# A latent attention's layer norm moved into the next stage's projection block, with contexts through a ring of three buffers

## The reference

```python
def _layernorm(x): (x - mean) * rsqrt(var + 1e-5)                     # no affine part

# fourth stage
x = _layernorm(x + latent_attention(x))

# fifth stage, its projections
q     = rms_norm(linear(x, q_w, q_b), norm_q_w)                       # x: 800 rows of 512
k     = rms_norm(linear(ctx_txt, k_w, k_b), norm_k_w)                 # context rows 257 to 360 of 8 batches
k_img = rms_norm(linear(ctx_img, k_img_w, k_img_b), norm_k_img_w)     # context rows 0 to 256
# then attention(q, k_img, v_img) + attention(q, k, v)

# sixth stage's weights, in bf16
scale = clip(mean(|w_g|), 1e-8)             # over 64 weights
q3    = clip(round(w_g / scale), -1, 1)
w     = w + (q3 * scale - w)                # both roundings to bf16 are kept
```

## Time and profile before

| | |
|---|---|
| median of 3 runs | 2397.46 us (2393.82 to 2399.54) |
| the profiled execution's own time | 2400.9 us |
| its span | 2399.2 us, 36927 instructions |
| TensorE matmul busy | 2210.1 us (92%) |
| VectorE, ScalarE, GpSimd busy | 1451.4, 1179.4, 471.3 us |

### The profile page before, as it was taken

How to read it: one execution, slowest core, us unless ns; L and a number is a source line. 1 busy time by engine, 2 the same in 40 slices (tenths; PEclk the granted TensorE clock), 3 DMA queues, 4 the chain that set the end, 5 groups by cost and what they waited for, 6 DMA issues and landing times. The chain is left out here.

```text
span 2399.2 us, 36927 instructions
## 1 busy us (share of the span) xinstructions
PE 2210.1 (92%) x13440; PEld 1735.9 (72%) x13440; DVE 1451.4 (60%) x3971; ACT 1179.4 (49%) x3034; POOL 471.3 (20%) x386
## 2 busy tenths in 40 slices
PE   7998899999998999899987988999996797998998
PEld 4643788888887888788876965665664594665987
DVE  2275677777776777677767535455553356883434
ACT  1052667576765676566752324452352244772222
POOL 0220122222221212122211002223232000221433
PEclk9999999999999999999998999999997998998999
DMA  6001211111101111111003023213220700002300
GB/s 230 1 34 66 76 36 36 36 37 36 37 35 37 36 37 34 38 36 36 10 5 141 1 73 119 96 72 115 102 75 27 250 1 19 2 2 87 125 1 28
DMA packets 46316, 135.58 MB, mean 57 GB/s; under 512 B 5527, under 2 KB 23959, under 8 KB 41143
## 3 DMA queue, kind: packets, MB, share of 16 engines
q1 hardware_dynamic: 34328, 112.00, 12.8%
q0 software_dynamic: 2304, 12.58, 1.3%
q10 hardware_dynamic: 9504, 8.65, 1.2%
HBM read 113.07 MB, written 20.15 MB: 56 GB/s over the span
## 5 line engine op out<-in xcount | busy, mean ns | idle before, releaser
L775 PE MATMUL psum<-qa_kv_raw,context 128*128 128x256 f32 (+1 forms) x1536 | 343.6, 380 | 0.0
L775 PEld LDWEIGHTS psum<-qa_kv_raw,context 128*128 128x128 f32 (+1 forms) x1536 | 277.2, 184 | 44.9
L761 PE MATMUL psum<-qa_w,qa_xq 128*100 128x256 bf16 (+1 forms) x3072 | 271.6, 249 | 19.1 <-issue 16.0
L761 PEld LDWEIGHTS psum<-qa_w,qa_xq 128*100 128x100 bf16 x3072 | 259.9, 128 | 21.0 <-issue 20.7
L877 ACT ACTIVATE qa_prob<-psum,qa_nm 100x361 f32<-100x361 f32 x128 | 71.8, 561 | 173.4 <-DVE qa_nm L1011 173.4
L1103 POOL TENSOR_TENSOR qa_w<-qa_w_raw,qa_w 128x768 bf16<-128x768 f32 x32 | 52.6, 1643 | 447.4 <-DVE qa_w L953 447.4
L973 DVE BATCH_NORM_STATS2 qa_st<-psum 100x6 f32<-100x128 f32 x320 | 69.6, 283 | 89.1 <-PE psum L761 89.1
L2395 ACT ACTIVATE it_prob<-psum,it_nm 100x257 f32<-100x257 f32 (+1 forms) x256 | 101.7, 412 | 42.6 <-DVE it_nm L2419 42.6
L832 PE MATMUL psum<-qa_catq,qa_o 128*128 128x400 f32 x512 | 111.9, 361 | 9.9 <-DVE X L1050 6.0
L2082 POOL TENSOR_TENSOR la_gf_diff<-la_gf_what,la_gf_w 128x1536 bf16<-128x1536 bf16 x16 | 49.3, 3083 | 306.4 <-DVE la_gf_what L1991 266.0
L1002 DVE TENSOR_SCALAR qa_nrm_t<-psum,qa_mv,qa_sd 100x128 f32<-100x128 f32 x320 | 107.8, 403 | 2.4
(11 more groups left out here) (345 smaller groups left out, 5093.5 us busy)
## 6 DMA issues: line engine op xcount, KB each, us to landing
qa_w_raw<-in_qa_w SPq DMA_DIRECT2D x9, 1536.0 KB, 6.8
la_gf_raw<-in_gf_w SPq DMA_DIRECT2D x16, 768.0 KB, 4.3
gf_ternary<-gf_made POOLq DMA_DIRECT2D x16, 768.0 KB, 3.6
gf_w<-gf_ternary SPq DMA_DIRECT2D x4, 3072.0 KB, 24.4
qa_piece<-in_tf_pieces ACTq DMA_DIRECT2D x66, 128.0 KB, 2.1
qa_o_raw<-in_qa_o SPq DMA_DIRECT2D x8, 1024.0 KB, 5.0
context<-in_context SPq DMA_DIRECT2D x8, 722.0 KB, 12.4
it_context<-in_context SPq DMA_DIRECT2D x8, 722.0 KB, 11.3
```

The costliest lines, as they stand in the source:

```text
L761: mm = pe.matmul(psum[0:T, 2 + at // 512, at % 512:at % 512 + width], xq[:, kind, k, b * T:(b + 1) * T], w3[:, s, part, k, at:at + width], ...
L775: mm = pe.matmul(psum[0:rows, i // 2, (i % 2) * 256:(i % 2) * 256 + 256], ctxT[:, k, b * TC + t0:b * TC + t0 + rows], kv_raw[:, s, k, :], ...
```

## The change

The separate block `ln_la` is dropped. Its mean, centring, squares, variance, root, reciprocal and multiplication are written at the head of the image-text projections' block, over halves (products, root, reciprocal) and quarters (the rest), with the centring in place in Y and the squares in `qn`. The order of the groups becomes k0, k1, q of tokens 0 to 399, k2 to k7, q of tokens 400 to 599, q of tokens 600 to 799. The contexts go through three buffers; the load of context b waits until the products of context b - 3 are done. SyncE queues the image key weights, context 0, the text key weights, context 1, then the query weights. In the latent attention, set 2's three steps follow additions 0, 1 and 2, set 3's scales follow additions 2, 3 and 4 (with the magnitude products placed likewise), and set 3's steps follow additions 5, 6 and 7, in every quad. The last quad's GpSimd does three sets; the two passes and the store of the sixteenth set move into the projections' block, behind the clearing of a row of v. Buffers that outlive the latent attention are in `LastGated`. The rest of the diff's core:

```diff
-                    if i in (0, 1, 3):
-                        ternary(g, 2, steps=((0, 1, 3).index(i),))
-                    if i in (2, 4, 6):
-                        take_scale(g, 3, i // 2 - 1, 5)
-                ternary(g, 3)
+                    if i < 3:
+                        ternary(g, 2, steps=(i,))
+                    if i in (2, 3, 4):
+                        take_scale(g, 3, i - 2, 5)
+                    if i >= 5:
+                        ternary(g, 3, steps=(i - 5,))
...
-            quad(QUADS - 1)
+            quad(QUADS - 1, 3)
...
+    RING = 3
+    groups = [("k", 0, 0, TC), ("k", 1, 0, TC), ("q", 0, 0, HALF)] + [("k", b, 0, TC) for b in range(2, B)] + [
+        ("q", 1, 0, QUARTER), ("q", 1, QUARTER, HALF)]
...
+            def load_context(b):
+                if b >= RING:
+                    sp.wait_ge(S_["kq_mm"], (ordinal(b - RING) + 1) * C)
+                sp.dma_start(ctxT[:, b % RING, :, :], a["context"][b]).then_inc(c_in[b % RING], 16)
+
+            sp.dma_start(w[1][:, :, :], a["it_ki"]).then_inc(S_["w_ki"], 16)
+            load_context(0)
+            sp.dma_start(w[2][:, :, :], a["it_kt"]).then_inc(S_["w_kt"], 16)
+            load_context(1)
             sp.dma_start(w[0][:, :, :], a["it_q"]).then_inc(S_["w_q"], 16)
...
             for b in range(B):
+                if b + 2 < B:
+                    load_context(b + 2)
                 sp.dma_start(v[:, b, 0:2, :], values[b, 0:2].rearrange("i p o -> p i o")).then_inc(S_["v_in"], 16)
...
+            sp.wait_ge(stored, 16 * FC)
...
+            mean(0)
+            mean(1)
+            variance(0)
+            variance(1)
...
+            act.activation(spare[:, :], core.eps[1.0], ACT.Sqrt)
+            for q in range(4):
+                act.wait_ge(S_["cen_ready"], q + 1)
+                act.activation(qn[:, :, quarter_of(q)], Y[:, :, quarter_of(q)], ACT.Square).then_inc(S_["ln_sq_ready"], 1)
+            for h in range(2):
+                act.wait_ge(S_["var_ready"], h + 1)
+                act.activation(std[:, half_of(h)], psum[:, 6 + h, 0:HALF], ACT.Sqrt, bias=core.eps[EPS]).then_inc(
+                    S_["std_ready"], 1)
...
             pool.memset(v[0:1, :, 2, :], 0.0)
+            pool.tensor_tensor(last.diff[:, :, :], last.what[:, :, :], last.gw[:, :, :], ALU.subtract).then_inc(
+                S_["last_diff"], 1)
+            pool.wait_ge(S_["last_diff"], 1)
+            pool.tensor_tensor(last.made[:, :, :], last.gw[:, :, :], last.diff[:, :, :], ALU.add).then_inc(
+                S_["last_made"], 1)
+            pool.wait_ge(S_["last_made"], 1)
+            pool.dma_start(scratch[QUADS - 1, 3], last.made[:, :, :].rearrange("p u o -> p (u o)").bitcast(F32)).then_inc(
+                stored, 16)
...
+            for q in range(4):
+                dve.wait_ge(S_["mean_ready"], q // 2 + 1)
+                mean = psum[:, 6 + q // 2, (q % 2) * QUARTER:(q % 2 + 1) * QUARTER]
+                dve.tensor_tensor(Y[:, :, quarter_of(q)], Y[:, :, quarter_of(q)], spread(mean), ALU.subtract).then_inc(
+                    S_["cen_ready"], 1)
+            for h in range(2):
+                dve.wait_ge(S_["std_ready"], h + 1)
+                dve.reciprocal(std[:, half_of(h)], std[:, half_of(h)]).then_inc(S_["ln_inv_ready"], 1)
+                dve.wait_ge(S_["ln_inv_ready"], h + 1)
+                for q in (2 * h, 2 * h + 1):
+                    dve.tensor_tensor(X[:, :, quarter_of(q)], Y[:, :, quarter_of(q)], spread(std[:, quarter_of(q)]),
+                                      ALU.mult).then_inc(S_["ln_normed"], 1)
```

More of the change, by code:

```diff
@@ L1643, with __init__, latent_attention_stage @@
 LA_SCALE = float(1.0 / np.sqrt(NOPE + ROPE))
-def latent_attention_stage(nc, core, a, Y, made, scratch, stored):
+class LastGated:
+    def __init__(self, nc, ctx):
+        self.gw, self.what, self.diff = (ctx.enter_context(nc.sbuf_tensor(f"gf_last_{x}", [P, 3, D], BF16))
+                                         for x in ("w", "what", "diff"))
+        self.made = ctx.enter_context(nc.sbuf_tensor("gf_last_made", [P, 3, D], F32R))
+def latent_attention_stage(nc, core, a, Y, last, scratch, stored):
     TIE = 0.5 + 2.0 ** -9
@@ new lines, in image_text_projections, with half_of, quarter_of, spread @@
+        c_in = [core.sem(f"itp_ctx{r}") for r in range(RING)]
+        block = ctx.enter_context(nc.Block())
+        def half_of(h):
+            return slice(h * HALF, (h + 1) * HALF)
+        def quarter_of(q):
+            return slice(q * QUARTER, (q + 1) * QUARTER)
+        def spread(t):
+            return t.unsqueeze(1).broadcast_to([P, C, QUARTER])
+        def width(g):
+            return g[3] - g[2]
+        def place(g):
+            return qn[:, :, g[1] * HALF + g[2]:g[1] * HALF + g[3]] if g[0] == "q" else kT[:, :, g[1], :]
@@ L2175, in _, with mean, variance @@
             sp.wait_ge(S_["v_in"], 32 * B)
+            sp.wait_ge(stored, 16 * FC)
         @block.tensor
         def _(pe):
+            def mean(h):
+                for c in range(C):
+                    mm = pe.matmul(psum[:, 6 + h, 0:HALF], core.avg[:, :], Y[:, c, half_of(h)], start=(c == 0), stop=(c == C - 1))
+                mm.then_inc(S_["mean_ready"], 1)
+            def variance(h):
+                pe.wait_ge(S_["ln_sq_ready"], 2 * h + 2)
+                for c in range(C):
+                    mm = pe.matmul(psum[:, 6 + h, 0:HALF], core.avg[:, :], qn[:, c, half_of(h)], start=(c == 0), stop=(c == C - 1))
+                mm.then_inc(S_["var_ready"], 1)
             def square_sum(n):
@@ L2213, in _ @@
                     for x0, x1, _, bias, _ in segments(g):
-                        last = act.activation(dest(g, c)[:, x0:x1], psum[:, (n * C + c) % 4, x0:x1], ACT.Identity,
+                        last = act.activation(place(g)[:, c, x0:x1], psum[:, (n * C + c) % 4, x0:x1], ACT.Identity,
                                               bias=core.param(bias, c))
@@ L2219, in _ @@
                     act.wait_ge(S_["ssq_mm"], n)
-                act.activation(sq[:, :, 0:width(g)], dest_all(g), ACT.Square).then_inc(S_["sq_ready"], 1)
+                act.activation(sq[:, :, 0:width(g)], place(g), ACT.Square).then_inc(S_["sq_ready"], 1)
                 if n:
-                    root(act, n - 1)
-            root(act, len(groups) - 1)
+                    root(n - 1)
+            root(len(groups) - 1)
         @block.gpsimd
```

123 lines of the change are left out of this document (52 added, 71 removed).

## The result

The changed kernel takes 2371.34 us, the median of 4 runs (2368.54 to 2383.0), against 2398.5 for the kernel before in the runs beside it. That is 27.2 us less by the medians, and 24.7 by the ratio, 0.9897 [0.9859, 0.9935], whose interval reaches from 15.6 to 33.8 us. The forecast was 2367.0 and 30.5 us less. The time lies in the forecast's range, 4.3 us above its middle.

The account below looks back on a forecast made before the run. TensorE's three holes around the norm, and a VectorE and ScalarE tail, were taken as the bound. Savings of 29.95 us to the first group plus 0.7 after, rounded to 30.5, from 2397.46 gave 2367.0 us; range 2361.0 to 2373.5.

Parts of the forecast that it names:

- Set 3's steps, -2.8: End of latent attention: only `sign_big` stays behind the last addition, so VectorE is done 2.8 us earlier.
- GpSimd's passes and the store, -11.4: Crossing after latent attention: the sixteenth set's passes and store leave the path, 12.4 us becoming 1.0.
- The norm in the projections' block, -8.3: Head of the projections' block: first group starts 11.2 us in, replacing the separate norm's 19.5 us.
- -0.7, -5.15, -1.6: Ahead of and in the first groups: second crossing removed, first weights' wait removed, slow half-clock start removed, in us.
- q first: Projections' group order: putting q ahead of k0 and k1 would cost 7 us.
- From the first group to the block's end: Projections' groups and tail: 99.1 us plus 27.2 us, 126.3 against 127.0 before, so -0.7 us.
- The clock: TensorE at the first crossing's new 2.5 us hole: full clock kept; the tail's 3 us hole left to Rival 1.
- Rival 1: Half clock behind the new holes at crossing and tail: +3 to +6 us, 2370 to 2373; chance 0.12.
- the loads: Projections' start: first contexts and weights land only 14 to 15 us in, +3 to +4 us, 2371; chance 0.06.
- contention: Norm's centring: VectorE and GpSimd hinder each other, at worst 6.2 us of waiting, 2373; chance 0.05.
- the ring: Projections' three context buffers: nothing late, 0; as rival, late contexts make it slower than before, 2398 and above, chance 0.015.
- the latent block still ending with a store: Latent attention's end: the fifteenth set's store keeps 5 us of the crossing, 2371; chance 0.03.

Follow-up runs that it names:

- e3: Changed kernel with set 2's and set 3's steps, scales and magnitude products back in their old places: 2372.02 us, ratio 0.9886 to the kernel before.
- e2: Changed kernel with the sixteenth set's GpSimd passes and store back in latent attention's block: 2378.34 us, ratio 0.9923 to the kernel before.
- e11: Changed kernel with the norm again in its own block ahead of the projections: 2391.7 us, ratio 0.9965 to the kernel before.
- e1: The changed kernel run again without an edit: 2373.48 us, ratio 0.9885 to the kernel before; changed stretch 145.0 us.
- e6: Changed kernel with both q groups ahead of the k groups and query weights loaded first: 2374.02 us, ratio 0.9899 to the kernel before.
- e4: Changed kernel with VectorE summing each group's squares ahead of finishing the previous group: 2363.46 us, ratio 0.9860 to the kernel before.
- e5: Changed kernel with four unread products added in the tail's hole ahead of the last square sum: 2373.71 us (2 runs), ratio 0.9895.
- e8: e4 with three unread products added behind latent attention's last product: 2364.77 us, ratio 0.9855 to the kernel before.
- e9: The kernel before run again without an edit: 2398.12 us, ratio 0.9995; changed stretch 172.3 us.
- e7: Changed kernel with two context buffers instead of three: 2369.87 us (2 runs), ratio 0.9879 to the kernel before.
- e10: e8 with four short unread products added in each of the last quad's last four batches: 2361.85 us, ratio 0.9852 to the kernel before.

## Why the prediction was right or wrong

**Where the time goes, and that it is faster**: right. 29.4 of 30.6 us stand in the changed stretch of the profiled execution.

**Set 3's steps, -2.8**: right; e3 gives back 2.8. The reordering inside the other quads costs nothing visible.

**GpSimd's passes and the store, -11.4**: right in its mechanism, and e2 gives back 10.9 of it. The crossing was mis-sized: 1.0 us taken from 0.7 and 0.8, 1.44 measured. +0.4. Why it is twice the other two is not shown; the prediction's reason, the number of semaphores, was not tested.

**The norm in the projections' block, -8.3, and -0.7, -5.15, -1.6**: right, and the time was lost in the places named. The first group started 11.28 us into the block (11.2 forecast) with no wait on a load; e11 gives back 16.2 us against e1 and 18.6 against the first trace, for the four terms' 15.75. Against e1 the three removals, e2, e3 and e11, give back 10.8, 2.9 and 16.2 us, 29.9 together, where e1's own gain in the stretch is 27.0; e11's longer wait for a load is half of what is over. Of the products' order the same passage said that q first "would cost 7 us": wrong, e6 shows 2.5 to 3.2. That sentence was in no term of the sum.

**From the first group to the block's end**: the groups 99.3 (99.1), the tail 27.7 (27.2), +0.7 together. The 200-column operations are near half of the 400-column ones, as taken (the multiplications 1.44 us for four). The hole ahead of the last q group was seen to a fifth of a microsecond. That it is a loss which VectorE's order can take away was not asked: e4 has 6.7 us there.

**The clock: the step that failed.** "The new hole at the first crossing is 2.5 us, ahead of which TensorE was busy, so I keep full clock." The hole is 2.96 us, since the crossing is longer, and in five of seven profiled executions the norm's mean products ran at half clock behind it, +1.7 us, where the prediction had put nothing; the first trace happened to be one of the two others. The row against it was the 5.61 us behind a hole of 1.52 us at the gated stage, and that row says nothing of a hole twice as long. The row for it was misread. The prediction says that the clock fell "3.3 us after 1985.75", but TensorE still did a square sum there, in the timeline of the kernel before:

```profile
1985.58 0.79 PE L2183 MATMUL psum<-itp_sq,ones 128*128 128x361 f32 x2
```

It ended at 1986.37, and the clock fell between 1989 and 1990, by the granted clock of 0.53 in that microsecond at its very start: 2.7 us after the last work, less than the hole of 2.96 us. Rival 1 with its 0.12 was thus the likely case and not the forecast, but its price of +3 to +6 us was too high: 1.7 at the crossing, and 0 to 0.7 in the tail, since VectorE's work hides the slower q group (e5).

**The sum put right.** -30.6 + 1.2 of mis-sized terms = -29.4 with the clock kept (as the trace of after has it), and -27.0 with the clock lost (e1's stretch, 172.0 - 145.0). From 2398.2, the median of the kernel before in the runs beside e1, the latter gives 2371.2; the ten runs of the changed kernel have a median of 2371.65. Of the 4.3 us between forecast and result 1.0 is the median of before, taken as 2397.46 from three runs where four gave 2398.5. The other 3.3 us are about the 1.2 of terms and the 2.4 of the clock, but this is an estimate: the timed runs have no trace, and steps of 5 us in latent attention lie on top of it, so that the close agreement is in part luck.

**The rivals that fell**: the loads (first group not held up), contention (centring 1.88 us with and without GpSimd's passes), the ring (nothing even with two buffers), the latent block still ending with a store (1.44 us, no trace of 5).

**What stays open**: why latent attention takes 404, 409 or 414 us in the same code. The granted clock over 1800 to 1812 is 0.57 to 0.82 in the traces of 409 us (before, e1, e3, e6, e11) and 1.00 in those near 404 (after, e2, e4, e8, e9, at the same place in the code); e5 and e7, at 414, have a second stretch of 0.74 and 0.76 at 1486 to 1498, where the others show 1.00. What decides it in a given execution was not found, and e10 couldn't show a cure. Open too is whether half clock near 1800 makes the clock fall behind the 2.96 us hole, with which it went together in seven of seven traces.

## What to carry to other kernels

A store or a pass of a slow engine at the end of a block is paid in full by every engine, with the crossing behind it; moved into the next block beside long work of TensorE it costs nothing (10.9 us here). Where two groups' elementwise work overlap at a tail, let VectorE do first what TensorE's next instruction waits for, and finish the older group after it: 6.7 us here for a reordered loop. And price the clock at each hole that a change leaves: a row from a hole half as long is no evidence, and one trace with the clock kept says only that it can be kept. An edit that seems to keep it has to be tried in executions of the kind that lost it.

## What the runs showed of the hardware

- A hole of 2.96 us on TensorE, behind unbroken work, was followed by half clock in five of seven executions of nearly the same code and by full clock in two, and the five were those with half clock some 20 us earlier as well. Behind a hole of 3.15 us in the tail, four of six lost it (after, e1, e7, e11) and two kept it (e2, e3). Holes of 1.46 us (twice) and 1.52 us (in all 13 traces) were followed by full clock, those of 5.75, 13.88 and 16.7 us by half clock. The Trainium skill (TensorE: Matmul & The Clock Gate, "Why this matters for your kernels") warns that idle gaps between bursts of products bring the half clock back; the traces agree for the long holes, and for those near 3 us in some executions and not in others.
- A block's end waits for GpSimd's store in flight: 5.2 us from the end of its issue to the next block, in the kernel before and in e2 alike, of which 3.0 us until the store has landed. Without a store in flight 0.7 to 1.44 us pass between two blocks.
- A program's time has steps of about 5 us from one execution to the next, which go together with stretches of half clock that an execution happens to have in latent attention (404, 409, 414 us). This is a larger part of the scatter than the changed stretch, which repeats to 0.3 us in the kernel before and to 2.4 us in the kernel after, by the clock at its holes.
